# The attended product of the first context attention as seven block products, with two general PSUM banks

## The chip, the cores and the metric

The kernel runs on one core of one Trainium2 chip. The metric is the device time of one execution in microseconds (us); lower is better. Five engines work side by side, each through its own instruction queue in program order: TensorE (PE; its weight loads are listed apart as PEld), VectorE (DVE), ScalarE (ACT), GpSimd (POOL) and SyncE (SP), which here only issues transfers. They synchronise by semaphores alone.

## What is computed

Two transformer layers over a state x of 8 batches x 128 tokens x 512. Each has an attention over a context (8 x 2048 x 512), a self attention and a feed-forward part. The change is in the first layer's context attention. Per batch and per head (8 heads, query and key width 64, value width 128):

```python
k = jnp.einsum('bkt,hta->bhka', key_tokens, key_down)
q = jnp.einsum('bqt,hta->bhqa', query_tokens, query_down) + query_down_bias[None]
logits = jnp.einsum('bhka,bhqa->bhkq', k, q)
attn = swishmax(logits, axis=-2)        # x*exp(x-max) / (sum|x*exp(x-max)| + 1)
vs = jnp.einsum('bhkq,bkt->bhqt', attn, key_tokens)
vs = jnp.einsum('bhqc,hct->bhqt', jnp.einsum('bhqt,htc->bhqc', vs, value_down), value_up)
return vs.sum(axis=1)
```

The fifth line, weights (keys x queries) times context tokens (keys x 512), is the attended product. All data is float32.

## The kernel before

`perceiver` runs one function per part of the layers, each a block of its own with one instruction stream per engine. `swishmax_context` is the first. It works in **units**: unit u is batch b = u // 4 and a pair of heads g = u % 4, 32 units in all (NU). Each unit has four **chunks** c of 512 keys, so there are 128 steps n = 4u + c. `pe_step`, `act_step` and `dve_step` write out by hand what each engine does in step n:

- `key` (for the next unit): keys of the pair from the transposed context, 4 matmuls of 512 columns into a general bank, copied out by ACT.
- `score`: 2 matmuls into two score banks of their own, one per head. DVE takes the maximum (`max`), ACT the exponential (`exp`), DVE multiplies by the score (`weigh`), ACT sums the absolute values (`abs`), DVE scales (`scale`).
- `turned` (for the unit before): the weights of each head are transposed, 4 transposes of 128 x 128 into a general bank. Head 0 is copied out by ACT, head 1 by DVE, into `weights_t`, which holds two chunks.
- `attend` (for the chunk of n - LAG, LAG = 5): the attended product of one chunk. For 4 key tiles k and 4 column tiles m a matmul takes the context tile as stationary operand and 256 columns of weights (two heads x 128 queries): 16 matmuls, accumulated over the four chunks in two banks `attended`.
- `values` (after the fourth chunk): ACT and DVE copy one `attended` bank each to `values_t`, after which the next unit's `attend` may start over.
- `inner` (once a unit): 8 matmuls of 128 columns with `value_down`; `output` (once a batch): 8 matmuls of 512 columns with `value_up`, which DVE adds to x. `hidden` and `query` prepare the queries of the next batch.

The order on PE inside a step is score, key, turned (both heads), inner where there is one, attend, and then hidden, query or output where there is one. The four general banks are handed out in turn by `SharedRing`: whoever fills a bank waits until what stood in it four places earlier has been copied out (`evicted(before)`). PSUM has eight banks: four general, two `attended`, two `score`.

In the profile a float32 matmul appears as two MATMUL and two LDWEIGHTS instructions, and a transpose as one of each; so the 16 matmuls of `attend` are x32. Context chunks are loaded by POOL into `context` (one batch, a chunk overwritten as soon as the last unit of the batch before has attended it), transposed context and weights by SP. All of `value_down` and `value_up` lie in SBUF.

After this stage come two self attentions (`token_attention`, called "twin" and "plain"), the experts, the second layer's context attention and the rest. In both self attentions some tiles `ahead` of the second context attention are computed first, from `ahead.stream` and `ahead.w`.

## Time and profile before

| | us |
|---|---|
| median of 3 runs | 4236.43 |
| lowest and highest run | 4236.34, 4237.85 |
| the profiled execution | 4237.23 |
| span of its trace, first to last instruction | 4235.4 |
| of it, first stage (swishmax_context) | 0 to about 1755 |

| engine | busy, us | share |
|---|---|---|
| PE | 4116.7 | 97% |
| PEld | 2772.9 | 65% |
| DVE | 1982.7 | 47% |
| ACT | 1402.7 | 33% |
| POOL | 240.6 | 6% |

A row of the timeline merges equal instructions that follow one another: its start, the time from the first start to the last end, the engine, the line, what is written and read, and their count (x). A PE row runs on for some hundredths to a tenth of a microsecond after the next has begun, because matmuls are pipelined; so the time from one row's start to the next row's start is what a piece of work takes on PE. "idle before" in square brackets is the engine's idle time ahead of a row and what ended it.

### The profile page before, as it was taken

The numbers are of one execution on the slowest core, as the hardware profiler recorded it, in microseconds if no ns is written. First come the engines' busy times: TensorE is split into PE (matmuls) and PEld (weight loads), VectorE is DVE, ScalarE is ACT, GpSimd is POOL, SyncE is SP. The second block draws the span as 40 slices with busy tenths as digits, with TensorE's granted clock in tenths as the row PEclk, the third lists the DMA queues.
The fourth block names the chain that finished last, engine by engine and source line by source line (L and its number), as shares of the span: only waits on it lengthen the run. The fifth ranks groups of instructions, "written<-read, shape, count | busy, mean of one in ns | idle before, by whom it ended". The sixth has DMA issues, their size and how long they took to land. (4 is left out here: it accounts for less than half of the span.)

```text
span 4235.4 us, 62228 instructions
## 1 busy us (share of the span) xinstructions
PE 4116.7 (97%) x25216; PEld 2772.9 (65%) x25216; DVE 1982.7 (47%) x4077; ACT 1402.7 (33%) x3796; POOL 240.6 (6%) x247
## 2 busy tenths in 40 slices
PE   9999999999999999999899999999999999999897
PEld 5767676767777677677466444666666666676675
DVE  4333333333333333245544233666666666656556
ACT  3222222222222222144333100444444444434343
POOL 0000000000000000012210000000000000000122
PEclk9999999999999999999999999999999999999999
DMA  5011111111111111201120500101101101101000
GB/s 180 30 49 32 40 40 40 40 40 40 40 40 40 40 40 40 85 21 41 54 90 22 184 0 25 50 15 53 45 24 53 43 26 53 43 11 43 11 2 21
DMA packets 86435, 189.71 MB, mean 45 GB/s; under 512 B 7696, under 2 KB 17552, under 8 KB 84368
## 3 DMA queue, kind: packets, MB, share of 16 engines
q1 hardware_dynamic: 72976, 137.55, 9.7%
...
q14 instruction: 71, 0.58, 0.0%
...
## 5 line engine op out<-in xcount | busy, mean ns | idle before, releaser
L502 PE MATMUL swishmax_attended<-swishmax_weights_t,swishmax_context 128*128 128x256 f32 x4096 | 905.1, 379 | 0.0
L502 PEld LDWEIGHTS swishmax_attended<-swishmax_weights_t,swishmax_context 128*128 128x128 f32 x4096 | 768.4, 190 | 99.2
L517 PE MATMUL swishmax_bank<-ahead_stream,swishmax_w_key 128*128 128x512 f32 x1024 | 474.9, 607 | 7.4 <-DMA ahead_stream<-in_context_t_dram 7.4
L1427 PE MATMUL context_bank<-ahead_stream,ahead_staged 128*128 128x512 f32 x1024 | 473.0, 605 | 1.3 <-PEq L1000 1.3
L1293 ACT ACTIVATE context_exps<-context_score,context_neg_max 128x512 f32<-128x512 f32 x512 | 344.7, 685 | 379.4 <-DVE context_neg_max L1325 379.4
L383 ACT ACTIVATE swishmax_xes<-swishmax_score,swishmax_neg_max 128x512 f32<-128x512 f32 x256 | 164.5, 687 | 836.4 <-DVE swishmax_neg_max L415 836.4
L517 PEld LDWEIGHTS swishmax_bank<-ahead_stream,swishmax_w_key 128*128 128x128 f32 x1024 | 184.9, 190 | 287.2 <-issue 284.1
L1427 PEld LDWEIGHTS context_bank<-ahead_stream,ahead_staged 128*128 128x128 f32 x1024 | 184.2, 189 | 280.8 <-issue 273.9
L415 DVE TENSOR_REDUCE swishmax_neg_max<-swishmax_score 128x1 f32<-128x512 f32 x256 | 165.0, 686 | 432.2 <-PE swishmax_score L488 432.2
L1325 DVE TENSOR_REDUCE context_neg_max<-context_score 128x1 f32<-128x512 f32 x512 | 317.8, 683 | 104.8 <-PE context_score L1395 104.1
L1442 PEld LDWEIGHTS context_bank<-whole_ident,context_exps 128*128 128x128 f32 x2048 | 229.1, 141 | 119.1 <-issue 69.5
L1442 PE MATMUL context_bank<-whole_ident,context_exps 128*128 128x128 f32 x2048 | 276.2, 277 | 17.7 <-ACT context_weights_t L1311 11.4
L1436 PE MATMUL context_bank<-ahead_w,ahead_stream 128*128 128x128 f32 x2304 | 269.0, 275 | 0.0
L1436 PEld LDWEIGHTS context_bank<-ahead_w,ahead_stream 128*128 128x128 f32 x2304 | 263.3, 192 | 1.9 <-issue 1.9
L1342 DVE TENSOR_SCALAR context_exps<-context_exps,context_scale 128x512 f32<-128x512 f32 x512 | 213.4, 481 | 1.1
L1311 ACT COPY context_weights_t<-context_bank 128x512 f32<-128x512 f32 x308 | 177.6, 588 | 105.8 <-PE context_bank L1442 104.8
L455 DVE COPY swishmax_weights_t<-swishmax_bank 128x512 f32<-128x512 f32 x128 | 88.5, 691 | 226.1 <-PE swishmax_bank L523 226.1
L420 DVE TENSOR_TENSOR swishmax_xes<-swishmax_xes,swishmax_score 128x512 f32<-128x512 f32 x256 | 164.6, 684 | 20.0 <-ACT swishmax_xes L383 20.0
L1363 DVE COPY context_weights_t<-context_bank 128x512 f32<-128x512 f32 x204 | 141.0, 691 | 48.9 <-PE context_bank L1442 34.2
L523 PEld LDWEIGHTS swishmax_bank<-whole_ident,swishmax_xes 128*128 128x128 f32 x1024 | 119.6, 141 | 66.7 <-issue 66.3
L391 ACT ACTIVATE swishmax_unused<-swishmax_xes 128x512 f32<-128x512 f32 x256 | 160.3, 636 | 0.0
L1395 PE MATMUL context_score<-context_keys_t,context_queries_t 32*128 32x512 f32 x1024 | 147.2, 645 | 0.9 <-DVE context_queries_t L1367 0.9
...
## 6 DMA issues: line engine op xcount, KB each, us to landing
ahead_stream<-in_context_t_dram SPq DMA_DIRECT2D x78, 1024.0 KB, 5.5
swishmax_context<-in_context_dram POOLq DMA_DIRECT2D x32, 1024.0 KB, 5.8
ahead_values<-ahead_staged SPq DMA_DIRECT2D x14, 1024.0 KB, 8.4
...
swishmax_up<-in_L_xattn_value_up_dram SPq DMA_DIRECT2D x1, 2048.0 KB, 10.1
```

The costliest lines, as they stand in the source:

```text
L383: nc.scalar.activation(xes[:, n % XES, r, :], score[r][:], ACT.Exp, bias=neg_max[:, e, r, c:c + 1]).then_inc(exped, 1)
L415: nc.vector.tensor_reduce(neg_max[:, e, r, c:c + 1], score[r][:], AX.X, ALU.max, negate=True).then_inc(maxed, 1)
L420: nc.vector.tensor_tensor(xe, xe, score[r][:], ALU.mult).then_inc(weighted, 1)
L502: last = nc.tensor.matmul(attended[m // 2][:, m % 2, :], context[:, c, k, m * P:(m + 1) * P], weights_t[:, n % 2, k].rearrange("p r q -> p ...
L517: last = nc.tensor.matmul(bank_t[:], w_key[:, k, g * P:(g + 1) * P], context_t[:, c, k, :], start=k == 0, stop=k == DC - 1)
L1293: nc.scalar.activation(exps[:, n % EXPS, r, :], score[r][:], ACT.Exp, bias=neg_max[:, u % 2, r, c:c + 1], accum_out=total[:, u % 2, r, c:c ...
L1311: nc.scalar.copy(weights_t[:, n % 2, r], ring.bank(t)[:].rearrange("p (k q) -> p k q", q=P)).then_inc(out_a, 1)
L1325: nc.vector.tensor_reduce(neg_max[:, e, r, c:c + 1], score[r][:], AX.X, ALU.max, negate=True).then_inc(maxed, 1)
L1342: nc.vector.tensor_scalar(exps[:, slot, r, :], exps[:, slot, r, :], scale[:, e, r, c:c + 1], None, ALU.mult).then_inc(scaled, 1)
L1427: last = nc.tensor.matmul(bank_t[:], w["k"][:, k, g * P:(g + 1) * P], context_t[:, c, k, :], start=k == 0, stop=k == DC - 1)
L1436: last = nc.tensor.matmul(bank_t[:, m * P:(m + 1) * P], context_t[:, c, k, m * P:(m + 1) * P], w["v"][:, k, g * P:(g + 1) * P], start=k == ...
L1442: last = nc.tensor.transpose(bank_t[:, k * P:(k + 1) * P], exps[:, n % EXPS, r, k * P:(k + 1) * P], ident[:])
```

## The change

**Seven products.** The weights of a chunk (512 keys x two heads of 128 queries) and the context (512 keys x 512 columns) are each cut into four blocks: key halves, heads, and halves of the columns. The four block outputs (two column halves x two heads) are formed from seven block products instead of eight (the Winograd form of Strassen's scheme). Each product is 2 key tiles x 2 column tiles, a matmul of 128 columns each: 28 matmuls of 128 columns in place of 16 of 256. They accumulate over the four chunks in four `attended` banks, two products to a bank and one in the last.

**Sums of the context** (S1, S2, S4 in a new tile `sides`, S3 in place of one quarter of `context`): four GpSimd instructions of 512 columns per chunk and batch, in `combine_sides`.

**Sums of the weights** (T1 to T4): in the `turned` step of DVE. The transposes are now grouped by head block so that ACT copies B11 and B21 and DVE reads B12 and B22 from its bank: one copy and four sums of 256 columns in place of one copy of 512.

**Sums of the products:** at the end of a unit ACT copies the first bank (products 1 and 2) to `pair`; GpSimd adds its halves (`first_value`), DVE does six sums of 256 columns. `values_t` has one buffer, not two.

**PSUM:** two general banks instead of four, since `attended` takes four. On PE the two `turned` of a step now stand on either side of `key`; on ACT `turned` stands between the two `exp`. `output` is done per unit (2 matmuls) one step after `inner`.

**SBUF:** to make room, `value_down` and `value_up` are loaded per unit in slabs of two heads (two slabs), the key weights lie in `ahead.w` and `ahead.w` itself is loaded near the end of the stage, and `xes` has 5 places, not 6. In both self attentions the weights share one semaphore, so the first query waits for all of them.

The diff, cut to its core:

```diff
+    KEYS, XES = 6, 5
+
+    A11, A12, A22, S1, S2, S3, S4 = range(7)
+    B11, B21, B22, T1, T3, T2, T4 = range(7)
+    PRODUCTS = ((A11, B11), (A12, B21), (S4, B22), (S1, T1), (S3, T3), (S2, T2), (A22, T4))
...
-        w_key = s.sb("w_key", [P, DC, H * A])
+        w_key = ahead.w
...
-        down = s.sb("down", [P, H, DC, C])
-        up = s.sb("up", [P, H, D])
+        down = s.sb("down", [P, 2, HG, DC, C])
+        up = s.sb("up", [P, 2, HG, D])
...
+        sides = s.sb("sides", [P, NCH, 3, 2, D // 2])
...
-        weights_t = s.sb("weights_t", [P, 2, DC, HG, P])
+        weights_t = s.sb("weights_t", [P, 2, 7, 2, P])
...
-        values_t = s.sb("values_t", [P, 2, DC, HG * P])
-        inner_t = s.sb("inner_t", [P, H, P])
+        values_t = s.sb("values_t", [P, DC, HG, P])
+        pair = s.sb("pair", [P, 2, 2, P])
+        partial = s.sb("partial", [P, 3, 2, P])
+        inner_t = s.sb("inner_t", [P, 2, HG, P])
...
-        bank = [s.ps(f"bank{n}", [P, CH]) for n in range(4)]
-        attended = [s.ps(f"attended{n}", [P, 2, HG * P]) for n in range(2)]
+        bank = [s.ps(f"bank{n}", [P, CH]) for n in range(2)]
+        attended = [s.ps(f"attended{n}", [P, 2, 2, P]) for n in range(4)]
...
+        def product(i):
+            return attended[i // 2][:, i % 2]
+
+        def side(which, c, k, m):
+            if which in (S1, S2, S4):
+                return sides[:, c, (S1, S2, S4).index(which), k, m * P:(m + 1) * P]
+            lower, right = which in (A12, A22), which in (A22, S3)
+            return context[:, c, 2 * lower + k, 2 * right * P + m * P:2 * right * P + (m + 1) * P]
...
-            out = [("key", 0, c + 1)] * (u == 0 and c + 1 < NCH) + [("score", u, c)] * (u < NU) + [("key", u + 1, c)] * (u + 1 < NU)
-            out += [("turned", u - 1, c, r) for r in range(HG)] * (1 <= u <= NU)
+            out = [("key", 0, c + 1)] * (u == 0 and c + 1 < NCH) + [("score", u, c)] * (u < NU)
+            out += [("turned", u - 1, c, 0)] * (1 <= u <= NU) + [("key", u + 1, c)] * (u + 1 < NU) + [("turned", u - 1, c, 1)] * (1 <= u <= NU)
             out += [("inner", (n - LAG) // NCH - 1)] * (n - LAG >= NCH and (n - LAG) % NCH == 0)
+            out += [("output", (n - LAG) // NCH - 1)] * (n - LAG >= NCH and (n - LAG) % NCH == 1)
             out += [("attend", (n - LAG) // NCH, (n - LAG) % NCH)] * (0 <= n - LAG < NU * NCH)
-            out += [("hidden", b + 1)] * (g == 2 and c == 1 and b + 1 < B) + [("query", b + 1)] * (g == 2 and c == 2 and b + 1 < B)
-            return out + [("output", b - 1)] * (g == 1 and c == 2 and b >= 1)
+            return out + [("hidden", b + 1)] * (g == 2 and c == 1 and b + 1 < B) + [("query", b + 1)] * (g == 2 and c == 2 and b + 1 < B)
...
-            out += [("exp", u, c, r) for r in range(HG)] * (u < NU) + [("key", u + 1, c)] * (u + 1 < NU)
-            out += [("turned", u - 1, c, 0)] * (1 <= u <= NU)
+            out += [("exp", u, c, 0)] * (u < NU) + [("turned", u - 1, c, 0)] * (1 <= u <= NU)
+            out += [("exp", u, c, 1)] * (u < NU) + [("key", u + 1, c)] * (u + 1 < NU)
...
+                def load_slab(u):
+                    g = u % NG
+                    for r in range(HG):
+                        sp.dma_start(down[:, u % 2, r], a["value_down"][HG * g + r].rearrange("(t p) c -> p t c", p=P)).then_inc(slab_landed[u % 2], 16)
+                    sp.dma_start(up[:, u % 2], a["value_up"][HG * g:HG * g + HG].rearrange("h c d -> c h d")).then_inc(slab_landed[u % 2], 16)
...
+                    if c == NCH - 1:
+                        if u >= 2:
+
+                            sp.wait_ge(full_d, ring.count(("output", u - 2)))
...
+                def combine_sides(b, c):
+                    pool.wait_ge(ctx_landed[c], 16 * (b + 1))
+                    a11, a12, a21 = context[:, c, 0:2, 0:2 * P], context[:, c, 2:4, 0:2 * P], context[:, c, 0:2, 2 * P:]
+                    a22 = context[:, c, 2:4, 2 * P:]
+                    s1, s2, s4 = (sides[:, c, n] for n in range(3))
+                    link(nc.gpsimd.tensor_tensor(s1, a21, a22, ALU.add))
+                    link(nc.gpsimd.tensor_tensor(s2, s1, a11, ALU.subtract))
+                    link(nc.gpsimd.tensor_tensor(s4, a12, s2, ALU.subtract))
+                    nc.gpsimd.tensor_tensor(a21, a11, a21, ALU.subtract).then_inc(sided, 1)
+
+                def first_value(u):
+                    pool.wait_ge(values_out_a, u + 1)
+                    nc.gpsimd.tensor_tensor(values_t[:, 0:2, 0, :], pair[:, 0], pair[:, 1], ALU.add).then_inc(values_out_p, 1)
+
                 for b in range(B):
-                    for c in range(NCH):
-                        if b:
-
-                            pool.wait_ge(attended_chunk, (b * NG - 1) * NCH + c + 1)
-                        else:
-                            pool.wait_ge(ctx_t_landed[NCH - 2], 16)
-                        pool.dma_start(context[:, c], ctx_dram[b * NCH + c].rearrange("(k p) d -> p k d", p=P)).then_inc(ctx_landed[c], 16)
+                    fetch(b, 0)
+                    fetch(b, 1)
+                    combine_sides(b, 0)
+                    fetch(b, 2)
+                    combine_sides(b, 1)
+                    fetch(b, 3)
+                    if b:
+                        first_value(b * NG - 1)
+                    combine_sides(b, 2)
+                    combine_sides(b, 3)
+                    for g in range(NG - 1):
...
-                        nc.scalar.copy(values_t[:, e, 0:2, :], attended[0][:]).then_inc(values_out_a, 1)
+                        nc.scalar.copy(pair[:], attended[0][:]).then_inc(values_out_a, 1)
...
-                        nc.vector.tensor_copy(values_t[:, e, 2:4, :], attended[1][:]).then_inc(values_out_d, 1)
+                        dve.wait_ge(values_out_a, u + 1)
+                        p3, p5, p7, p6, p4 = (product(i) for i in range(2, 7))
+                        u2, u3, u4 = (partial[:, i] for i in range(3))
+                        link(nc.vector.tensor_tensor(u2, pair[:, 0], p6, ALU.add))
+                        nc.vector.tensor_tensor(u3, u2, p7, ALU.add)
+                        link(nc.vector.tensor_tensor(u4, u2, p5, ALU.add))
+                        nc.vector.tensor_tensor(values_t[:, 0:2, 1, :], u4, p3, ALU.add)
+                        nc.vector.tensor_tensor(values_t[:, 2:4, 0, :], u3, p4, ALU.subtract)
+                        nc.vector.tensor_tensor(values_t[:, 2:4, 1, :], u3, p5, ALU.add).then_inc(values_out_d, 1)
...
-                            n, r = u * NCH + t[2], t[3]
-                            last = nc.vector.tensor_copy(weights_t[:, n % 2, :, r, :], ring.bank(t)[:].rearrange("p (k q) -> p k q", q=P))
+                            n = u * NCH + t[2]
+                            w = weights_t[:, n % 2]
+                            b12, b22 = (ring.bank(t)[:, 2 * h * P:2 * (h + 1) * P].rearrange("p (k q) -> p k q", q=P) for h in range(2))
+                            link(nc.vector.tensor_copy(w[:, B22], b22))
+                            dve.wait_ge(out_a, ring.count(("turned", u, t[2], 0)))
+                            nc.vector.tensor_tensor(w[:, T1], b12, w[:, B11], ALU.subtract)
+                            link(nc.vector.tensor_tensor(w[:, T3], w[:, B22], b12, ALU.subtract))
+                            dve.sem_inc(out_d, 1)
+                            link(nc.vector.tensor_tensor(w[:, T2], w[:, B22], w[:, T1], ALU.subtract))
+                            nc.vector.tensor_tensor(w[:, T4], w[:, T2], w[:, B21], ALU.subtract).then_inc(combined, 1)
+                            continue
...
-                        evicted(("turned", u, c, 1))
-                        pe.wait_ge(ctx_landed[c], 16 * (b + 1))
+                        pe.wait_ge(combined, n + 1)
+                        pe.wait_ge(sided, b * NCH + c + 1)
...
-                        for k in range(DC):
-                            for m in range(DC):
-                                last = nc.tensor.matmul(attended[m // 2][:, m % 2, :], context[:, c, k, m * P:(m + 1) * P],
-                                                        weights_t[:, n % 2, k].rearrange("p r q -> p (r q)"),
-                                                        start=c == 0 and k == 0 and m % 2 == 0,
-                                                        stop=c == NCH - 1 and k == DC - 1 and m % 2 == 1)
+                        for i, (left, right) in enumerate(PRODUCTS):
+                            for k in range(2):
+                                for m in range(2):
+                                    last = nc.tensor.matmul(product(i)[:, m, :], side(left, c, k, m), weights_t[:, n % 2, right, k, :],
+                                                            start=c == 0 and k == 0 and m == 0 and i % 2 == 0,
...
-                        pe.wait_ge(values_out_a, u + 1)
+                        pe.wait_ge(values_out_p, u + 1)
...
-                        evicted(("inner", u * NG + NG - 1))
-                        pe.wait_ge(ahead.w_loaded, 32)
-                        for h in range(H):
-                            last = nc.tensor.matmul(bank_t[:], inner_t[:, h, :], up[:, h, :], start=h == 0, stop=h == H - 1)
+                        evicted(("inner", u))
+                        for r in range(HG):
+                            last = nc.tensor.matmul(bank_t[:], inner_t[:, u % 2, r, :], up[:, u % 2, r, :], start=r == 0, stop=r == HG - 1)
...
-                        pe.wait_ge(w_loaded[what[0]], 16)
+                        pe.wait_ge(w_loaded, w_loads)
+                        if twin and what == "query":
```

How the instructions stand, word for word. TensorE, unit 0's `inner` step, the kernel before:

```order
L488 MATMUL swishmax_score<-swishmax_keys_t,swishmax_queries_t 128x512 x2
L517 MATMUL swishmax_bank<-ahead_stream,swishmax_w_key 128x512 x4
L523 MATMUL swishmax_bank<-whole_ident,swishmax_xes 128x128 x8
L530 MATMUL swishmax_bank<-swishmax_values_t,swishmax_down 128x128 x8
L502 MATMUL swishmax_attended<-swishmax_weights_t,swishmax_context 128x256 x16
```

and the same step of the changed kernel (here a matmul and a transpose count once each):

```order
L603 MATMUL swishmax_bank<-whole_ident,swishmax_xes 128x128 x4
L597 MATMUL swishmax_bank<-ahead_stream,ahead_w 128x512 x4
L603 MATMUL swishmax_bank<-whole_ident,swishmax_xes 128x128 x4
L610 MATMUL swishmax_bank<-swishmax_values_t,swishmax_down 128x128 x8
L583 MATMUL swishmax_attended<-swishmax_weights_t,swishmax_context 128x128 x8
L583 MATMUL swishmax_attended<-swishmax_weights_t,swishmax_sides 128x128 x8
L583 MATMUL swishmax_attended<-swishmax_weights_t,swishmax_context 128x128 x4
L583 MATMUL swishmax_attended<-swishmax_weights_t,swishmax_sides 128x128 x4
L583 MATMUL swishmax_attended<-swishmax_weights_t,swishmax_context 128x128 x4
```

Half of the transposes now stand between `key` and `inner`, where all of them stood before, and the 16 matmuls of 256 columns have become 28 of 128.

VectorE from the last `scale` of a unit's fourth attended chunk to the next step, before:

```order
L438 TENSOR_SCALAR swishmax_xes<-swishmax_xes,swishmax_scale 128x512 x2
L442 COPY swishmax_values_t<-swishmax_attended 128x512
L415 TENSOR_REDUCE swishmax_neg_max<-swishmax_score 128x1 x2
L420 TENSOR_TENSOR swishmax_xes<-swishmax_xes,swishmax_score 128x512 x2
L455 COPY swishmax_weights_t<-swishmax_bank 128x4x128
```

and in the changed kernel:

```order
L506 TENSOR_TENSOR swishmax_partial<-swishmax_pair,swishmax_attended 128x256
L507 TENSOR_TENSOR swishmax_partial<-swishmax_partial,swishmax_attended 128x256
L508 TENSOR_TENSOR swishmax_partial<-swishmax_partial,swishmax_attended 128x256
L509 TENSOR_TENSOR swishmax_values_t<-swishmax_partial,swishmax_attended 128x2x128
L510 TENSOR_TENSOR swishmax_values_t<-swishmax_partial,swishmax_attended 128x2x128
L511 TENSOR_TENSOR swishmax_values_t<-swishmax_partial,swishmax_attended 128x2x128
L476 TENSOR_REDUCE swishmax_neg_max<-swishmax_score 128x1 x2
L481 TENSOR_TENSOR swishmax_xes<-swishmax_xes,swishmax_score 128x512 x2
L526 COPY swishmax_weights_t<-swishmax_bank 128x256
L528 TENSOR_TENSOR swishmax_weights_t<-swishmax_bank,swishmax_weights_t 128x256
L529 TENSOR_TENSOR swishmax_weights_t<-swishmax_weights_t,swishmax_bank 128x256
L531 TENSOR_TENSOR swishmax_weights_t<-swishmax_weights_t 128x256
```

One copy between two steps has become six sums ahead of the next step's maxima, and one copy of the turned weights a copy and four sums.

## Rows read from the trace of the kernel before

**Rows 1.** The page: busy time, share and instructions; granted clock in 40 slices.

```profile
PE 4116.7 (97%) x25216; PEld 2772.9 (65%) x25216; DVE 1982.7 (47%) x4077; ACT 1402.7 (33%) x3796; POOL 240.6 (6%) x247
...
PEclk9999999999999999999999999999999999999999
```

**Rows 2.** Windows: from:to length, busy us (x) per engine, clock, DMA share, GB/s.

```profile
60.00:1744.00 1684.00, 1683.75 (x7393) 1193.83 (x7392) 593.69 (x1192) 462.23 (x1047) 20.97 (x28) 1.00 0.12 38
1744.00:4235.40 2491.40, 2381.75 (x17664) 1554.93 (x17664) 1363.22 (x2822) 920.92 (x2708) 216.26 (x211) 0.98 0.13 43
```

**Rows 3.** The page's groups: busy us, mean ns of one, idle before.

```profile
L502 PEld LDWEIGHTS swishmax_attended<-swishmax_weights_t,swishmax_context 128*128 128x128 f32 x4096 | 768.4, 190 | 99.2
```

**Rows 4.** Timeline of PE: start us, us, engine, line, what, count; an inner step.

```profile
697.79 1.13 PE L488 MATMUL swishmax_score<-swishmax_keys_t,swishmax_queries_t 64*128 64x512 f32 x4
698.85 3.70 PE L517 MATMUL swishmax_bank<-ahead_stream,swishmax_w_key 128*128 128x512 f32 x8
...
702.39 1.04 PE L523 MATMUL swishmax_bank<-whole_ident,swishmax_xes 128*128 128x128 f32 x8
703.26 1.95 PE L530 MATMUL swishmax_bank<-swishmax_values_t,swishmax_down 128*128 128x128 f32 x16
705.05 7.07 PE L502 MATMUL swishmax_attended<-swishmax_weights_t,swishmax_context 128*128 128x256 f32 x32
712.05 1.13 PE L488 MATMUL swishmax_score<-swishmax_keys_t,swishmax_queries_t 64*128 64x512 f32 x4
```

**Rows 5.** Timeline of ACT in the same step.

```profile
697.90 0.58 ACT L397 COPY swishmax_values_t<-swishmax_attended 128x512 f32<-128x512 f32 x1 [5.48 <-PE swishmax_attended L502]
699.67 1.29 ACT L383 ACTIVATE swishmax_xes<-swishmax_score,swishmax_neg_max 128x512 f32<-128x512 f32 x2 [1.19 <-DVE swishmax_neg_max L415]
702.59 0.59 ACT L400 COPY swishmax_keys_t<-swishmax_bank 128x512 f32<-128x512 f32 x1 [1.63 <-PE swishmax_bank L517]
703.07 0.59 ACT L404 COPY swishmax_weights_t<-swishmax_bank 128x512 f32<-128x512 f32 x1
```

**Rows 6.** Timeline of DVE, the end of this step and the start of the next.

```profile
705.25 0.43 DVE L458 COPY swishmax_inner_t<-swishmax_bank 128x256 f32<-128x256 f32 x1 [1.09 <-PE swishmax_bank L530]
705.59 0.87 DVE L438 TENSOR_SCALAR swishmax_xes<-swishmax_xes,swishmax_scale 128x512 f32<-128x512 f32 x2
713.21 1.29 DVE L415 TENSOR_REDUCE swishmax_neg_max<-swishmax_score 128x1 f32<-128x512 f32 x2 [6.75 <-PE swishmax_score L488]
714.65 1.28 DVE L420 TENSOR_TENSOR swishmax_xes<-swishmax_xes,swishmax_score 128x512 f32<-128x512 f32 x2 [0.16 <-ACT swishmax_xes L383]
```

**Rows 7.** Timeline of PE: long runs of 128-column matmuls in later stages.

```profile
1789.05 7.38 PE L916 MATMUL twin_bank_a<-twin_hidden_t,ahead_stream 128*128 128x128 f32 x64 [0.83 <-ACT ahead_staged L762]
1796.27 7.31 PE L916 MATMUL twin_bank_d<-twin_hidden_t,twin_wk 128*128 128x128 f32 x64
...
3054.16 3.84 PE L1452 MATMUL context_bank<-context_hidden_t,ahead_staged 128*128 128x128 f32 x32
3057.93 1.14 PE L1395 MATMUL context_score<-context_keys_t,context_queries_t 32*128 32x512 f32 x8
```

**Rows 8.** Groups of POOL, shapes apart: busy us, mean ns | idle before.

```profile
L862 POOL TENSOR_TENSOR plain_hidden<-plain_hidden,plain_offset 128x512 f32<-128x512 f32 x8 | 13.1, 1643 | 0.6
...
L871 POOL TENSOR_TENSOR twin_result<-twin_result,twin_gain 128x512 f32<-128x512 f32 x8 | 10.1, 1265 | 49.2 <-DVE twin_result L145 49.2
```

**Rows 9.** Timeline at the end of the first stage, PE and DVE.

```profile
1744.85 2.02 PE L530 MATMUL swishmax_bank<-swishmax_values_t,swishmax_down 128*128 128x128 f32 x16 [0.99 <-DVE swishmax_values_t L442]
...
1743.90 0.69 DVE L442 COPY swishmax_values_t<-swishmax_attended 128x512 f32<-128x512 f32 x1 [13.12 <-PE swishmax_attended L502]
```

**Rows 10.** The plain self attention: last weight load (issue, landing) and first query.

```profile
2112.53 2.29 SPq L191 DMA_DIRECT2D plain_wo<-in_L_ffn_Wo_dram  x1
...
plain_wo<-in_L_ffn_Wo_dram SPq DMA_DIRECT2D x1, 1024.0 KB, 15.0
...
2136.26 3.81 PE L916 MATMUL plain_bank_a<-plain_hidden_t,plain_wq 128*128 128x128 f32 x32 [0.83 <-ACT ahead_staged L762]
```

84 lines of the change are left out of this document (50 added, 34 removed).

## The prediction

> **What bounds the kernel now.** I read the page first: PE is busy for 97% of the span at full granted clock in practically every slice [rows 1]. Then a table by stage: in the steady part of the first stage, 60 to 1744 us, PE is busy 1683.75 of 1684.00 us, while DVE has 594, ACT 462 and POOL 21 us of work [rows 2]. So there PE waits for nobody, and the stage lasts as long as PE's own instructions follow one another. What PE is spared there is gained whole, and what it must wait for that it need not wait for now is lost whole. Then the timeline of one step, for the price of each piece as the time from its start to the next piece's start [rows 4]: score 1.06 us (697.79 to 698.85), key 3.54 (to 702.39), the eight transposes 0.87 (to 703.26), inner 1.79 (to 705.05), attend 7.00 (to 712.05). Last the same step on ACT and DVE, for where they stand when PE will need them [rows 5, 6].
>
> **The product.** It takes 7.00 us for 32 instructions of 256 columns, 0.219 each [rows 4]. The new one is 28 matmuls, 56 instructions of 128 columns. For that form the nearest rows are: 16 in 1.79 us in inner, 0.112 each [rows 4]; 64 in 7.22 us (1789.05 to 1796.27), 0.1128 each; 32 in 3.77 us (3054.16 to 3057.93), 0.1178 each [rows 7]. The new run is 56 long and unbroken, so the run of 64 is its nearest relative: 56 x 0.1128 = 6.32 us. The saving is 0.68 us a step, times 128 steps = **-87.0 us**; by the other two it would be 0.73 (-93) and 0.40 (-51). An eighth fewer columns would be 0.87 us; the rest is lost because the shorter matmul pays more beside its columns.
>
> **The sums of the weights.** DVE's part of turned grows from one copy of 512 to one copy and four sums of 256 columns. The row for 256 columns is 0.43 us [rows 6], four to five of them with their waits about 2.2 us. The chunk attended in a step is the one turned a step before, so a whole attend, over 6 us, lies between. DVE is idle for 6.75 us at the end of such a step [rows 6]. Cost 0. If that cover were gone, each further microsecond would be one on PE, 128 times.
>
> **Two general banks.** This is where PE starts to wait. With four banks nobody met one that was not yet copied out. With two, inner needs the bank that key filled two places before, and so does output a step later; the transposes and the next key find banks that were copied out long before. From rows: ACT starts the key copy 3.74 us after key starts (698.85 to 702.59) and takes 0.59 [rows 4, 5]; with some 0.06 us to wake PE (estimate from gaps between a copy's end and its follower) the bank is free 4.39 us after key's start. PE arrives after key and half of the transposes, 3.54 + 0.44 = 3.98. It waits 0.41 us, in 32 inner and 32 output steps: 64 x 0.40 = **+25.6 us**. Lower bound 0 (if the wait vanished in the pipeline), upper bound 0.5 each, +32, if PE must also reload a weight that it could not fetch ahead.
>
> **The sums of the products.** After a unit's fourth chunk DVE now has six sums where it had one copy, all ahead of the next step's maxima, and behind the maxima hang exp on ACT, then ACT's turned, exp and key copies. With time 0 at the start of the next score: ACT's copy of the pair runs from 0.11 (697.90 less 697.79) to 0.70 [rows 4, 5]. The first sum starts at 0.73. A dependent 256-column operation follows after about 0.46 us, an independent one after 0.34 (0.43 less the overlap of about 0.09 that the pair of 0.48 us scales in 0.87 us shows [rows 6]), so two dependent and four independent steps give 2.28 us, and the first max starts at 3.01 instead of 1.16 (713.21 less 712.05 [rows 4, 6]). Then exp of head 0 at 3.73, ACT's turned copy 4.33 to 4.92, second exp 4.83 to 5.52, key copy 5.42 to 6.00, PE woken at 6.06. PE wants the bank of the second half of the transposes at 1.06 + 0.44 + 3.54 = 5.04, which is free at 4.98: no wait, by a hair. It wants the key bank for inner at 5.48: it waits 0.58 us and not 0.40. So 32 x 0.18 = **+5.8 us**. The sums themselves (end 3.1) and GpSimd's (one addition of 256 columns, under 1.3 us, since 512 take 1.27 [rows 8]) are due at 5.48 and are hidden.
>
> **Sums of the context.** Four POOL instructions of 512 columns at 1.27 to 1.64 us [rows 8], 5 to 6.6 us a chunk, 32 chunks. They start when a chunk has landed; attend of that chunk of the new batch is four steps, some 50 us, after the buffer came free. Queued behind them on POOL are the next fetch and `first_value`; the fetch of chunk 3 waits for the last attend anyway, and `first_value` stands ahead of the last two chunks' sums. Cost 0; up to +10 us in all if a DVE chain is disturbed at the seven batch ends. Here the 1.64 us row shows one thing: the same POOL addition took 0.38 us longer than its twin of 1.27 in another phase. The Trainium skill (SBUF — State Buffer, Who interferes with whom) says that VectorE and GpSimd share a pair of ports and that one of them blocks wholly while a two-port VectorE instruction runs. Taken at its word a scale of DVE could stand still for one whole POOL instruction; this is 1.3 us against 6.75 idle, so the sum by that rule stays the same, except in the product sums, whose operands come partly from PSUM.
>
> **The rest.** Output is cut into 32 runs of 4 instructions where it had 8 runs of 16: the same columns, and some 0.1 us at 24 more seams, **+2.4**. At the end of the stage PE waits 0.99 us for one DVE copy that starts at 1743.90 [rows 9]; now it waits for the pair copy and the sums, 0.04 + 0.59 + 0.03 + 2.4 + 0.06 = 3.1 us: **+2.2**. The turned split around key keeps the number of seams: 0, at most 0.1 x 128 = 13. The slab loads have two units' time. Weight loads under one semaphore: in the plain phase the last is issued at 2112.53 and lands 15.0 us later, at 2128, and the first query runs at 2136.26 [rows 10]: 8 us of cover by the tiles ahead; cost 0.
>
> **Sum:** -87.0 + 25.6 + 5.8 + 2.4 + 2.2 = **-51 us**. The profiled execution took 4237.2 (span 4235.4), 0.8 over the median; 4237.2 - 51 = 4186.2, and against the median **4185 us**, -1.2%.
>
> **Rivals.**
>
> *A: the two banks cost nothing.* Then only seams remain: -87 + 5 = -82, 4154 us. For it: 0.4 us is a small figure, put together from starts and ends. Against: the key copy cannot start before key has ended, and only 0.44 us of transposes follow.
>
> *B: the product sums hold up the second transposes (slower).* The place is the step after each unit's last attend. The bank that ACT's turned copy frees is due at 5.04 and free at 4.98, so every microsecond by which DVE's chain is longer than reckoned goes to PE, 32 times. If all six sums went at the pace of dependent 512-column ones (0.69 + 0.04), the chain would be 4.4 us instead of 2.28, +2.1 x 32 = +67 us: 4252. It is level when the chain takes 1.6 us more, and slower by over 0.2% from 1.9 us more. For it: several waits stand in the chain, and POOL works beside it. Against: 256 columns took 0.43 us, not 0.69 [rows 6]. A chain 0.5 to 1 us longer gives 4200 to 4217.
>
> *C: the weight loads pace the product.* A weight load record lasts 190 ns [rows 3], and the new product has 56 of them instead of 32, each over a matmul of half the length. If they did not overlap, a product would take 56 x 0.19 = 10.6 us, +3.6 x 128, some 4650 us. The point of no gain is 0.125 us an instruction. The runs of 64 contradict it: same loads, 0.1128 [rows 7]. The Trainium skill (TensorE: Matmul & The Clock Gate, Back-to-back issue gap) says that the spacing of matmuls is set by the weight load as well and that short ones suffer, which speaks against this change; by that rule its time would be this rival's, but the rows above are of this very form.
>
> That the change doesn't do what it says is excluded by the order of the instructions.
>
> **How the numbers follow.** The forecast, with bank waits of 0.2 to 0.6 us, 4168 to 4200: chance 0.62. A, 4150 to 4168: 0.12. The milder B, 4200 to 4228: 0.14. B in full: 0.07, of it 0.03 within 0.2% and 0.04 slower. C: 0.02. The rest 0.03, something in the start of the stage or in GpSimd's sums, on the slower side as often as level. The range leaves out the ends of A, the upper part of mild B, full B and C: **4154 to 4216**. What a measurement of this kernel can tell from no change is about 0.2%, 8.5 us. Faster by more 0.88, within 0.05, slower 0.07.
>
> **What would show it.** From one attend row's start to the next row's start 6.3 us (over 7.0 is C). Idle time of PE ahead of inner and output, ended by ACT's key copy, 0.4 to 0.6 us each, 64 times; none is A. Idle time ahead of the second transposes, ended by ACT's turned copy, is B. The first max after a unit 3.0 us after the score's start. PE's wait ahead of the last inner 3 us. The granted clock stays at 2.4 GHz in the stage; drops after the new waits would make the prediction wrong, and so would a wait ended by POOL.

## The result and the profile after

The changed kernel takes 4212.49 us (median of 5 runs, 4211.15 to 4213.39) against 4236.57 us (5 runs, 4236.34 to 4239.4): ratio 0.9942, 95% interval 0.9931 to 0.9952. It is 24.1 us faster; 51 were forecast, with a range down to 21. The direction came out and the size did not, and the profile says where the other half stayed.

The page of the profile after, its first line and the two groups of the product (answering [rows 1, 3]; the product now reads either context tiles or the sums in `sides`):

```profile
PE 4053.0 (96%) x28288; PEld 2813.3 (67%) x28288; DVE 2247.2 (53%) x4773; ACT 1401.1 (33%) x3796; POOL 427.8 (10%) x407
...
L583 PE MATMUL swishmax_attended<-swishmax_weights_t,swishmax_context 128*128 128x128 f32 x4096 | 522.1, 276 | 0.0
...
L583 PE MATMUL swishmax_attended<-swishmax_weights_t,swishmax_sides 128*128 128x128 f32 x3072 | 385.5, 275 | 0.0
```

PE is busy 64 us less, but the span shrank by only 26 (4235.4 to 4209.3). So PE now waits, in a kernel where it waited almost nowhere. Windows of the first stage show in which stretches (columns as in [rows 2]: from:to, length, busy us of PE, PEld, DVE, ACT and POOL, granted clock, DMA share, GB/s):

```profile
60.00:69.00 9.00, 3.87 (x12) 1.61 (x10) 8.37 (x31) 0.93 (x2) 0.00 (x0) 0.96 0.00 0
69.00:76.00 7.00, 6.71 (x36) 6.71 (x37) 3.89 (x9) 2.53 (x7) 0.00 (x0) 0.57 0.00 1
...
82.00:1681.00 1599.00, 1575.99 (x10137) 1191.84 (x10136) 834.08 (x1825) 453.41 (x1032) 186.56 (x170) 1.00 0.19 61
1681.00:1690.00 9.00, 6.57 (x45) 6.36 (x44) 5.41 (x14) 1.07 (x2) 0.73 (x1) 0.81 0.00 0
...
1717.00:1740.00 23.00, 17.26 (x46) 9.11 (x44) 11.88 (x43) 1.13 (x3) 0.72 (x1) 0.70 0.20 74
```

The long middle has 23 us of idle PE, spread over 1599. The first row has 5 us in 9, and the clock of the next one, 0.57, says that PE spent most of it at the lower level (1.2 of 2.4 GHz). The end of the stage repeats this twice. To turn windows into a balance I took the starts of `score` on PE, one a step, and cut both stages at the same steps (the 9th and the 121st score; the first matmul of the next stage as the end). The last column is what the prediction's own terms give for each stretch.

| stretch | before, us | after, us | difference | due by the forecast |
|---|---|---|---|---|
| start to 9th score | 91.1 | 102.4 | +11.3 | -2.0 |
| 9th to 121st score | 1523.1 | 1479.0 | -44.0 | -46.7 |
| 121st score to end of stage | 141.6 | 149.3 | +7.7 | -2.4 |
| all later stages | 2479.7 | 2478.6 | -1.0 | 0 |
| sum | 4235.4 | 4209.3 | -26.1 | -51.1 |

Due are 3, 112 and 13 `attend` of -0.68 us, and the bank waits, seams and the end's wait where they fall. The steady part is right within 3 us. Two short stretches, together 6% of the kernel, ate 23 us.

**The steady step.** Timeline of PE (start, us, engine, line, what, count, [idle before <- releaser]); first a plain step, then the piece of an inner step around its wait, answering [rows 4]:

```profile
724.69 1.13 PE L568 MATMUL swishmax_score<-swishmax_keys_t,swishmax_queries_t 64*128 64x512 f32 x4
725.75 0.66 PE L603 MATMUL swishmax_bank<-whole_ident,swishmax_xes 128*128 128x128 f32 x4
726.24 3.60 PE L597 MATMUL swishmax_bank<-ahead_stream,ahead_w 128*128 128x512 f32 x8
729.67 0.60 PE L603 MATMUL swishmax_bank<-whole_ident,swishmax_xes 128*128 128x128 f32 x4
730.11 1.95 PE L583 MATMUL swishmax_attended<-swishmax_weights_t,swishmax_context 128*128 128x128 f32 x16
...
736.46 1.13 PE L568 MATMUL swishmax_score<-swishmax_keys_t,swishmax_queries_t 64*128 64x512 f32 x4
...
753.22 0.64 PE L603 MATMUL swishmax_bank<-whole_ident,swishmax_xes 128*128 128x128 f32 x4
754.27 2.05 PE L610 MATMUL swishmax_bank<-swishmax_values_t,swishmax_down 128*128 128x128 f32 x16 [0.41 <-ACT swishmax_keys_t L461]
756.16 1.95 PE L583 MATMUL swishmax_attended<-swishmax_weights_t,swishmax_context 128*128 128x128 f32 x16
```

From score to score it is 11.77 us where it was 12.47 (14.26 less the 1.79 of inner [rows 4]), so a plain step gains 0.70; `attend` takes 6.35 (730.11 to 736.46), forecast 6.32. An inner step takes 14.27 where it took 14.26: it gains 0.70 and loses 0.71 beyond its 1.79, ahead of line 610. An output step takes 13.99: 2.22 over a plain step, where its share of the matmuls is 1.72 (a quarter of the 6.87 that an output took in the kernel before), so it loses 0.50.

**Who waits for whom.** PE's waits after, 57 to 1735 us (engine, buffer and line that wait <- what they wait for: us in all, times, longest):

```profile
PE swishmax_bank L610 <- ACT swishmax_keys_t L461: 11.8, 29, 0.4
PE swishmax_bank L627 <- ACT swishmax_keys_t L461: 6.9, 29, 0.2
PE swishmax_bank L610 <- DVE swishmax_values_t L511: 5.7, 2, 3.3
PE swishmax_bank L603 <- ACT swishmax_weights_t L465: 5.6, 2, 5.4
PE swishmax_bank L610 <- ACT swishmax_weights_t L465: 2.8, 1, 2.8
PE swishmax_bank L603 <- DVE swishmax_xes L499: 2.1, 2, 1.8
```

The first two rows are the waits that the prediction named: ACT's key copy, 29 times each instead of 32. The rest are few and long, and they belong to the two short stretches.

**The start.** PE after, the sixth step, and below it what DVE and ACT did meanwhile:

```profile
59.81 0.63 PE L603 MATMUL swishmax_bank<-whole_ident,swishmax_xes 128*128 128x128 f32 x4 [1.76 <-DVE swishmax_xes L499]
60.27 3.60 PE L597 MATMUL swishmax_bank<-ahead_stream,ahead_w 128*128 128x512 f32 x8
69.29 1.12 PE L603 MATMUL swishmax_bank<-whole_ident,swishmax_xes 128*128 128x128 f32 x4 [5.42 <-ACT swishmax_weights_t L465]
70.20 3.62 PE L583 MATMUL swishmax_attended<-swishmax_weights_t,swishmax_context 128*128 128x128 f32 x16
73.61 2.62 PE L583 MATMUL swishmax_attended<-swishmax_weights_t,swishmax_sides 128*128 128x128 f32 x16
...
59.97 4.25 DVE L158 BATCH_NORM_STATS2 swishmax_x_stats<-whole_x 128x6 f32<-128x512 f32 x7
...
67.35 1.29 DVE L476 TENSOR_REDUCE swishmax_neg_max<-swishmax_score 128x1 f32<-128x512 f32 x2
...
68.08 0.69 ACT L441 ACTIVATE swishmax_xes<-swishmax_score,swishmax_neg_max 128x512 f32<-128x512 f32 x1 [9.67 <-DVE swishmax_neg_max L476]
68.66 0.58 ACT L465 COPY swishmax_weights_t<-swishmax_bank 128x512 f32<-128x512 f32 x1
```

Read it from below: PE's second transposes (69.29) want the bank that ACT empties at 68.66; ACT does that after exp of head 0 (68.08), which needs DVE's maximum (67.35), and ahead of that DVE computes the normalization statistics of batches 1 to 7 in one piece, 59.97 to 67.35. PE stands still for 5.42 us, and then runs 16 instructions in 3.41 us (70.20 to 73.61) and the next 16 in 2.46, where 1.79 is the pace at full clock. The step takes 21.92 us where it took 12.97; the one before it 8.63 where it took 6.19, since transposes now stand ahead of key and wait for a scale.

**The end.** PE after, the waits of the last two units (the middle ones left out), answering [rows 9]:

```profile
1646.52 2.05 PE L610 MATMUL swishmax_bank<-swishmax_values_t,swishmax_down 128*128 128x128 f32 x16 [2.82 <-ACT swishmax_weights_t L465]
...
1685.43 3.14 PE L610 MATMUL swishmax_bank<-swishmax_values_t,swishmax_down 128*128 128x128 f32 x16 [2.44 <-DVE swishmax_values_t L511]
...
1721.36 3.75 PE L610 MATMUL swishmax_bank<-swishmax_values_t,swishmax_down 128*128 128x128 f32 x16 [3.31 <-DVE swishmax_values_t L511]
1725.72 3.75 PE L627 MATMUL swishmax_bank<-swishmax_up,swishmax_inner_t 128*128 128x512 f32 x4 [0.61 <-DVE swishmax_inner_t L535]
```

In the last unit there is no key for a next one, and after it no score. So the 3.5 us of key that had covered the chain pair copy, sums, maxima, exp, turned copy are gone, while the chain is as long as before. The last wait of 3.31 us was forecast as 3.1; that the next 20 instructions would run at half clock, twice 3.75 us for what takes 1.95 and 1.9, was not.

### The profile page after: what moved, and what is told of

The parts are those of the page before. It is cut to its first block and busy times, and to the rows that moved or that the text cites. A ratio compares the mean times of both kernels' runs of the same rounds, so it can differ in the third digit from the quotient of the medians.

```text
span 4209.3 us, 69698 instructions
## 1 busy us (share of the span) xinstructions
PE 4053.0 (96%) x28288; PEld 2813.3 (67%) x28288; DVE 2247.2 (53%) x4773; ACT 1401.1 (33%) x3796; POOL 427.8 (10%) x407
## 5 line engine op out<-in xcount | busy, mean ns | idle before, releaser
L583 PE MATMUL swishmax_attended<-swishmax_weights_t,swishmax_context 128*128 128x128 f32 x4096 | 522.1, 276 | 0.0
L583 PEld LDWEIGHTS swishmax_attended<-swishmax_weights_t,swishmax_context 128*128 128x128 f32 x4096 | 492.7, 193 | 14.8 <-issue 14.8
L597 PE MATMUL swishmax_bank<-ahead_stream,ahead_w 128*128 128x512 f32 x1024 | 463.8, 596 | 7.6 <-DMA ahead_stream<-in_context_t_dram 7.6
L441 ACT ACTIVATE swishmax_xes<-swishmax_score,swishmax_neg_max 128x512 f32<-128x512 f32 x256 | 177.3, 694 | 843.2 <-DVE swishmax_neg_max L476 843.2
L583 PE MATMUL swishmax_attended<-swishmax_weights_t,swishmax_sides 128*128 128x128 f32 x3072 | 385.5, 275 | 0.0
L583 PEld LDWEIGHTS swishmax_attended<-swishmax_weights_t,swishmax_sides 128*128 128x128 f32 x3072 | 364.4, 192 | 0.0
L597 PEld LDWEIGHTS swishmax_bank<-ahead_stream,ahead_w 128*128 128x128 f32 x1024 | 185.8, 191 | 196.8 <-issue 194.6
L481 DVE TENSOR_TENSOR swishmax_xes<-swishmax_xes,swishmax_score 128x512 f32<-128x512 f32 x256 | 175.6, 687 | 66.8 <-ACT swishmax_xes L441 66.8
L603 PE MATMUL swishmax_bank<-whole_ident,swishmax_xes 128*128 128x128 f32 x1024 | 161.0, 281 | 10.8 <-ACT swishmax_weights_t L465 5.6
## 6 DMA issues: line engine op xcount, KB each, us to landing
whole_x<-in_x_dram SPq DMA_DIRECT2D x8, 256.0 KB, 10.9
```

Of the source, the lines that this page charges most:

```text
L441: nc.scalar.activation(xes[:, n % XES, r, :], score[r][:], ACT.Exp, bias=neg_max[:, e, r, c:c + 1]).then_inc(exped, 1)
L481: nc.vector.tensor_tensor(xe, xe, score[r][:], ALU.mult).then_inc(weighted, 1)
L583: last = nc.tensor.matmul(product(i)[:, m, :], side(left, c, k, m), weights_t[:, n % 2, right, k, :], start=c == 0 and k == 0 and m == 0 a ...
L597: last = nc.tensor.matmul(bank_t[:], w_key[:, k, g * P:(g + 1) * P], context_t[:, c, k, :], start=k == 0, stop=k == DC - 1)
L603: last = nc.tensor.transpose(bank_t[:, k * P:(k + 1) * P], xes[:, n % XES, r, k * P:(k + 1) * P], ident[:])
```

## The experiments

Two theories stood at the start. **Cover**: the loss is PE waiting for chains on DVE and ACT at the two ends, since with two banks transposes, inner and output meet a bank still in use; moving work on DVE or PE gives it back. **Contention**: GpSimd's sums, or the product itself, cost something in every step. All runs share the runs of the kernel before made in the same batch (medians 4236.7 to 4238.2).

**Statistics out of the way.** DVE gathers the statistics of batches 1 to 7 a step after the first `attend`, finishes them one step later, and the normalizations follow them.

```diff
-            out += [("stats", 1)] * (n == NCH) + [("norm", b + 1)] * (g == 1 and c == 2 and b + 1 < B)
+            out += [("gather", 1)] * (n == NCH + 2) + [("finish", 1)] * (n == NCH + 3) + [("norm", b + 1)] * (g == 2 and c == 0 and b + 1 < B)
```

> The changed kernel, but the row statistics of batches 1 to 7 on DVE (7.4 us in one piece, between steps 4 and 5) are cut in two and put behind steps 6 and 7; norm of batch 1 follows two steps later. Theory start-and-end (the 128-step middle went as forecast, the missing 27 us stand at the start and the end of the stage): PE's wait of 5.4 us ahead of the second transposes at 69.3 us and the half-clock stretch behind it go, 8 to 10 us less than 4212.5, so about 4203. Rival spread (GpSimd and DVE contention or seams in every step): 4212, no change.

4204.57 us (4202.6 to 4206.21), ratio 0.9924 (0.9908 to 0.9941), 7.9 faster than the change. PE in the step of the long wait:

```profile
61.11 3.60 PE L602 MATMUL swishmax_bank<-ahead_stream,ahead_w 128*128 128x512 f32 x8
64.55 0.60 PE L608 MATMUL swishmax_bank<-whole_ident,swishmax_xes 128*128 128x128 f32 x4
64.99 1.95 PE L588 MATMUL swishmax_attended<-swishmax_weights_t,swishmax_context 128*128 128x128 f32 x16
```

The second transposes follow key at once, the product's first 16 instructions take 1.95 instead of 3.62, and the step takes 13.57 instead of 21.92. The mechanism is shown. The total needs more care: the 9th score comes 7.5 us earlier, which is 8.35 from this step and 1.6 from a first score that happens to start earlier, less 2.45 in the step before it (11.08 instead of 8.63; the run without GpSimd's sums, below, shows where part of that comes from). The moved normalization makes seven steps 0.46 longer (15.17 instead of 14.71), and the stage ends only 2.9 earlier. Of the 8.5 between the two spans the other 5.6 lie in later stages whose instructions are the same; the section on the hardware comes back to them.

**Inner and output behind attend.** On PE they follow `attend` in their step, on DVE their copies follow the scales.

```diff
-            out += [("inner", (n - LAG) // NCH - 1)] * (n - LAG >= NCH and (n - LAG) % NCH == 0)
-            out += [("output", (n - LAG) // NCH - 1)] * (n - LAG >= NCH and (n - LAG) % NCH == 1)
             out += [("attend", (n - LAG) // NCH, (n - LAG) % NCH)] * (0 <= n - LAG < NU * NCH)
+            out += [("inner", (n - LAG) // NCH - 1)] * (n - LAG >= NCH and (n - LAG) % NCH == 0)
+            out += [("output", (n - LAG) // NCH - 1)] * (n - LAG >= NCH and (n - LAG) % NCH == 1)
```

> The changed kernel, but inner and output stand behind attend on PE (and behind scale on DVE), so that the key bank has long been copied out when they want it. Bank-wait theory: an inner step loses 0.7 us and an output step 0.48 us beyond their matmuls, 31 times each, 36 us in all, plus 2.8 + 0.95 + some of 2.4 us near the end of the stage; these go: 4170 to 4176. Rival: the wait only moves, to the next step's key or transposes, which then find the bank of inner or output not yet copied out: 4205 to 4215.

4172.74 us (4171.59 to 4174.61), ratio 0.9848 (0.9832 to 0.9864), 39.8 faster than the change. PE's waits, 82 to 1640 us, are all that is left there:

```profile
PE swishmax_attended L583 <- DVE swishmax_values_t L511: 1.1, 1, 1.1
PE swishmax_bank L603 <- DVE swishmax_xes L499: 0.4, 1, 0.4
PE swishmax_bank L603 <- ACT swishmax_weights_t L465: 0.2, 1, 0.2
```

An inner step now takes 13.60 and an output step 13.49; 32 times the 0.67 and the 0.50 saved is 37. In the last unit the steps take 11.47 and 10.05 instead of 13.21 and 11.26. So the bank waits are the whole loss of the steady part, and 6.3 us of product in front of inner are enough to hide ACT's key copy and DVE's chain both.

**Both.** The two edits together.

> Both edits, statistics moved and inner and output behind attend. If both theories hold and the parts are independent: the sum of their gains, 4160 to 4168, 1.7% under the kernel before. Rival: as the better of the two alone.

4162.68 us (4160.21 to 4169.94), ratio 0.983 (0.9813 to 0.9846). The sum of the two single gains, 47.7, gives 4164.8: they add. This version beats both kernels; the next ones only polish it.

**A short chain.** Three of the six sums of products on DVE are left out.

```diff
-                        link(nc.vector.tensor_tensor(u2, pair[:, 0], p6, ALU.add))
-                        nc.vector.tensor_tensor(u3, u2, p7, ALU.add)
-                        link(nc.vector.tensor_tensor(u4, u2, p5, ALU.add))
-                        nc.vector.tensor_tensor(values_t[:, 0:2, 1, :], u4, p3, ALU.add)
-                        nc.vector.tensor_tensor(values_t[:, 2:4, 0, :], u3, p4, ALU.subtract)
-                        nc.vector.tensor_tensor(values_t[:, 2:4, 1, :], u3, p5, ALU.add).then_inc(values_out_d, 1)
+                        nc.vector.tensor_tensor(values_t[:, 0:2, 1, :], pair[:, 0], p3, ALU.add)
+                        nc.vector.tensor_tensor(values_t[:, 2:4, 0, :], pair[:, 0], p4, ALU.subtract)
+                        nc.vector.tensor_tensor(values_t[:, 2:4, 1, :], pair[:, 0], p5, ALU.add).then_inc(values_out_d, 1)
```

> The changed kernel with three of the six DVE sums of the products left out (u2, u3, u4; the three that write the values stay, so part of the computation is missing). The chain ahead of the next maxima is 1.3 us shorter. Forecast's term: PE's wait ahead of inner falls from 0.41 to 0.24 us, 31 times, 5 us, and 1.3 us at each of the waits near the end: about 4204. Rival that the sums cost nothing because inner waits for the key copy anyway: 4210 to 4212. Rival that the chain is the main loss: under 4195.

4202.57 us (4199.89 to 4203.75), ratio 0.9919 (0.9902 to 0.9936). An inner step takes 14.06 instead of 14.27, and the first step of the last unit without key 11.96 instead of 13.21. With the sums shorter the inner step gives back 0.21 us, the 0.18 that the prediction had charged for them; its other 0.5 stays, and is the bank's. Where key is missing PE gets back 1.25 us, about the length of three sums: the waits of 2.82, 2.44 and 3.31 us at the end become 1.57, 1.19 and 2.06. The stretch from the 121st score to the end of the stage takes 141.8 us instead of 149.3. Of these 7.5 us the waits are 3.75; nearly all of the rest is that the clock stays up behind them, and that much happens without the shorter chain too, in the run without GpSimd's sums below.

**Before with two banks.** The kernel before, with two general banks and the order of the change on PE and ACT, the product as it was.

```diff
-        bank = [s.ps(f"bank{n}", [P, CH]) for n in range(4)]
+        bank = [s.ps(f"bank{n}", [P, CH]) for n in range(2)]
...
-            out += [("turned", u - 1, c, r) for r in range(HG)] * (1 <= u <= NU)
+            out += [("turned", u - 1, c, 0)] * (1 <= u <= NU) + [("key", u + 1, c)] * (u + 1 < NU) + [("turned", u - 1, c, 1)] * (1 <= u <= NU)
```

> The kernel before, with two general banks instead of four and the changed kernel's order on PE and ACT (transposes on both sides of key, turned between the exps); the product stays as it was, inner ahead of attend, output behind it once a batch. Theory start-and-end: 32 inner waits of 0.4 to 0.7 us (13 to 22 us) and 8 to 14 us at the start and end of the stage behind DVE's statistics and ACT's copies: 4260 to 4270. Rival, that the start and end losses come from the longer sums and not from the banks: 4250 to 4255.

4255.96 us (4250.54 to 4257.19) against 4236.7, ratio 1.0044 (1.0027 to 1.006). The long wait at the start is there, to the hundredth, without any product of seven:

```profile
67.20 1.12 PE L523 MATMUL swishmax_bank<-whole_ident,swishmax_xes 128*128 128x128 f32 x4 [5.42 <-ACT swishmax_weights_t L404]
68.11 9.05 PE L502 MATMUL swishmax_attended<-swishmax_weights_t,swishmax_context 128*128 128x256 f32 x32
```

The product behind it takes 9 us instead of 7.00, and the 9th score comes at 102.0 instead of 91.1. So 10.9 of the 13.3 us that the start lost against the forecast come from the banks and their order alone. An inner step takes 14.72 instead of 14.26, +0.46; over a plain step of the same kernel (12.43) and its 1.79 it is 0.50, for the bank alone, forecast 0.40. The end is another matter: from the 121st score to the end of the stage this kernel takes 143.3 us, only 1.7 over the kernel before, where the change takes 7.7 more. The total lies between the two expectations, nearer the rival's, and each was half right: the start is the banks', and the end needs the longer sums too.

**Before with 128 columns.** The kernel before, each matmul of the product split in two, so 64 instructions of 128 columns instead of 32 of 256.

```diff
-                                last = nc.tensor.matmul(attended[m // 2][:, m % 2, :], context[:, c, k, m * P:(m + 1) * P],
-                                                        weights_t[:, n % 2, k].rearrange("p r q -> p (r q)"),
...
+                                for r in range(HG):
+                                    last = nc.tensor.matmul(attended[m // 2][:, m % 2, r * P:(r + 1) * P], context[:, c, k, m * P:(m + 1) * P],
+                                                            weights_t[:, n % 2, k, r, :],
...
```

> The kernel before, each attend matmul of 256 columns cut in two of 128: 32 matmuls, 64 instructions, nothing else. Pace of the forecast, 0.111 to 0.113 us an instruction: attend 7.15 to 7.2 us in place of 7.0, 4255 to 4263. Rival that a long run of short matmuls is paced by weight loads (0.118 and more): over 4300.

4267.6 us (4264.53 to 4271.41) against 4236.7, ratio 1.0073 (1.0056 to 1.009), above what was expected. One product:

```profile
702.81 7.31 PE L503 MATMUL swishmax_attended<-swishmax_weights_t,swishmax_context 128*128 128x128 f32 x64
710.05 1.13 PE L488 MATMUL swishmax_score<-swishmax_keys_t,swishmax_queries_t 64*128 64x512 f32 x4
```

64 instructions in 7.24 us are 0.1131 each; 7.24 less 7.00, 128 times, is 30.7, all of the 30.9 measured. An eighth of 7.24 is 0.905, and 7.24 less 0.905 is 6.34, the `attend` of the change. This splits the product's -0.66 cleanly: +0.24 for the shorter form, -0.90 for the eighth product.

**Without GpSimd's sums.** They run for batch 0 only.

```diff
+                    if b:
+                        pool.sem_inc(sided, 1)
+                        return
                     s1, s2, s4 = (sides[:, c, n] for n in range(3))
```

> The changed kernel with GpSimd's sums of the context left out for batches 1 to 7 (those batches use the sums of batch 0; part of the computation is missing). Forecast: they are hidden and disturb nobody: 4212, within 2 us. Rival contention (DVE and GpSimd share ports at each batch end): 4 to 10 us less.

4212.07 us (4209.94 to 4213.31), ratio 0.9943 (0.9927 to 0.996); the change has 4212.49. Some 144 us of GpSimd work are gone and no step of batches 1 to 7 is shorter. So contention costs PE nothing there. But it exists, on DVE. The change at the first batch end, DVE, then one of GpSimd's four additions beside it, and last the DVE row of the same sum without GpSimd's:

```profile
282.65 1.38 DVE L532 TENSOR_TENSOR swishmax_weights_t<-swishmax_weights_t 128x256 f32<-128x256 f32 x1
284.28 2.56 DVE L499 TENSOR_SCALAR swishmax_xes<-swishmax_xes,swishmax_scale 128x512 f32<-128x512 f32 x2
...
282.41 1.33 POOL L409 TENSOR_TENSOR swishmax_sides<-swishmax_sides,swishmax_context 128x512 f32<-128x512 f32 x1
...
283.21 0.42 DVE L535 TENSOR_TENSOR swishmax_weights_t<-swishmax_weights_t 128x256 f32<-128x256 f32 x1
```

At each of the seven batch ends two sums of the weights take 1.2 to 1.5 and 1.4 us (the last time 0.7 and 1.4) instead of 0.42, and two scales 2.56 instead of 0.87, 2.9 to 3.7 us in all; the sums that read PSUM keep their 0.42. DVE is idle for 2.19 us behind it where it was idle for 5.92, and so PE sees nothing of it.

At the start it does. There batch 0's sums, which this run keeps, meet the chain of small DVE operations that the first transposes wait for: the sum into `total` takes 0.61 us in the change and 1.25 here, and the second operation after it 0.17 and 1.11, where the kernel before takes 0.17 for each; they end when the GpSimd addition beside them ends. PE's wait ahead of these transposes is 2.63 us in the kernel before with two banks, which has no such sums, 3.07 in the change, 3.84 with the statistics moved and 4.65 here, and the step takes 11.64 here instead of 8.63. No run of the changed kernel leaves out the sums of batch 0, so their direct price in the change, 0.44 us, is only read from these waits.

The stretches say what the median hides. From the 9th to the 121st score both kernels take 1479.0 us. But the stage ends in 145.7 us here and in 149.3 in the change, with the same instructions and the same waits of 2.82, 2.4, 3.31 and 0.61 us: behind the last two, inner and output take 2.02 and 1.95 us here and 3.75 and 3.75 in the change. The later stages then take 3.1 us more here (2481.7 for 2478.6). So whether the clock falls behind the last waits is not decided by these waits.

**The normalization back.** Both edits, and the normalization moved only in batch 0, where it has to follow the statistics.

```diff
-[("norm", b + 1)] * (g == 2 and c == 0 and b + 1 < B)
+[("norm", b + 1)] * (g == (1 if b else 2) and c == (2 if b else 0) and b + 1 < B)
```

> The kernel with both edits (statistics moved, inner and output behind attend), but norm back in its old step for all batches except batch 1, for which the statistics are too late there. With both edits the inner step that also has hidden takes 14.49 us where it took 14.03 with norm in its old step. If this is norm's 0.54 us ahead of the sums of the products, six steps get 0.46 us shorter: 2.8 us less than 4162.7, about 4160. If it is the split statistics or something of the step itself: no change.

4161.8 us (4161.27 to 4164.58), ratio 0.9824 (0.981 to 0.9837). Six steps take 14.03 instead of 14.49, 2.8 us; 0.9 of it is seen in the median, within the spread of the other's runs.

**A fill for the clock.** The same, and 28 transposes whose result nobody reads, while PE waits for the last sums.

```diff
                     elif what == "inner":
+                        if u == NU - 1:
+                            for k in range(28):
+                                nc.tensor.transpose(score[0][:, 0:P], ident[:], ident[:])
                         pe.wait_ge(values_out_p, u + 1)
```

> The same kernel, and on PE 28 transposes of the identity into a score bank that nobody reads any more, between the last attend and the last inner, where PE waits 3.3 us for the sums of the products; they take 28 x 0.109 = 3.05 us and write nothing that is used. Clock theory: it is this idle time that brings TensorE to 1.2 GHz behind it, where the last inner and output and the start of the next stage run at half speed; with the wait filled the clock stays at 2.4 GHz there and 4 to 6 us go, about 4155. Rival, that the clock falls anyway because of the pauses of 0.6, 1.2 and 0.8 us at the change of stage: within 1 us of the kernel without them.

4160.35 us (4159.47 to 4161.23), ratio 0.9819 (0.9805 to 0.9832), the fastest of all. The same place without the fill, timeline of PE and a window:

```profile
1677.67 3.75 PE L615 MATMUL swishmax_bank<-swishmax_values_t,swishmax_down 128*128 128x128 f32 x16 [3.31 <-DVE swishmax_values_t L511]
1682.03 3.75 PE L632 MATMUL swishmax_bank<-swishmax_up,swishmax_inner_t 128*128 128x512 f32 x4 [0.61 <-DVE swishmax_inner_t L540]
```

```profile
1673.00:1690.00 17.00, 11.88 (x37) 7.33 (x36) 6.42 (x14) 0.59 (x1) 0.73 (x1) 0.61 0.11 29
```

And with it:

```profile
1673.52 3.22 PE L612 MATMUL swishmax_score<-whole_ident 128*128 128x128 f32 x28
1676.83 2.02 PE L618 MATMUL swishmax_bank<-swishmax_values_t,swishmax_down 128*128 128x128 f32 x16
1679.46 1.96 PE L635 MATMUL swishmax_bank<-swishmax_up,swishmax_inner_t 128*128 128x512 f32 x4 [0.61 <-DVE swishmax_inner_t L540]
```

```profile
1674.00:1690.00 16.00, 13.82 (x62) 8.00 (x59) 10.44 (x34) 0.30 (x1) 0.73 (x1) 1.00 0.19 56
1690.00:1700.00 10.00, 7.88 (x15) 3.44 (x16) 2.02 (x10) 1.75 (x4) 0.00 (x0) 0.83 0.97 389
```

The fill fills the wait exactly and the clock stays at 2.4 GHz in this profile: 2.02 and 1.96 instead of 3.75 twice, and from the last run of the product to the first matmul of the next stage 10.00 us instead of 13.67. But of these 3.7 only 1.5 arrive in the median. In the next stage PE waits 2.39 us at 1692, and the clock falls there instead (0.83 in the last row). The second piece of that stage starts 9.5 us after the first with the fill, without it, in the change and in the kernel before: it waits for ACT. Without the fill the first piece runs at half clock, 8.71 us, and the wait is 0.80; with it the first piece takes 7.11 and the wait is 2.39, and from there to the next transposes it is 22.40 us instead of 20.70. So the half clock in the first piece had cost nothing, and its absence makes a longer wait with a drop behind it. The drop was put off, not removed. That the fill is what keeps the clock up is not shown: without GpSimd's sums and without any fill the same two rows are 2.02 and 1.95, behind the same wait of 3.31, and there too the next stage has a wait of 2.41. The median, 1.5 us lower, is all that speaks for the fill. The expectation counted the start of the next stage among what would be gained and had no place for that.

## Why the prediction was wrong in size

**Right.** The bound: PE without waits, so that what it is spared is gained. The product's price, 6.32 forecast and 6.27 to 6.35 measured, from the run of 64 in another stage [rows 7]. The chain of the sums: first max 3.01 us after the score forecast, 3.04 measured (748.23 to 751.27). The sums of the weights and GpSimd's at nothing, from batch 1 on: a scale of DVE does stand still for a GpSimd addition, as the prediction had allowed for, and so do sums of the weights, which it had not; 2.19 us of DVE's idle time are left over it. The bank waits: each step that was named lost what was charged within 0.13 us (inner 0.71 for 0.58; output 0.50 for 0.50, of it 0.10 for a seam). Together -44.0 in the middle for -46.7 due. As a rate, -0.393 a step, or -50.3 over 128 steps: the forecast's sum would be right for a stage that is all middle.

**The step that failed first** is the sentence in *Two general banks*: "the transposes and the next key find banks that were copied out long before". It was worked out in one steady step and applied to all. With two banks the second transposes need the bank of the first, which ACT empties behind exp, so behind DVE's maxima. In the steady step this chain ends 1.9 us before PE comes back from key (ACT's copy ends at 739.51, the transposes start at 741.45). At the start DVE has a single piece of 7.4 us ahead of the maxima. Before it stood on DVE too, and cost nothing, since four banks let PE go on. The price is 13.3 us against what was due: 8.35 in the step that the moved statistics take from 21.92 to 13.57, 2.4 in the step before it, 1.3 more in the same step, where the transposes now stand ahead of key and wait 1.76 us for a scale, and 1.3 in the first score. That last part is chance: its start differs by as much between kernels with the same work ahead of it (22.66, and 21.05 with the statistics moved). The kernel before with two banks shows 10.9. Rival B named exactly this chain, "the second transposes wait for ACT's turned copy", but looked for it behind the product sums, 32 times, and not behind the one long piece of DVE's work. The start was mentioned only as part of a rest of 0.03.

**The second** is the term *end of the stage*, +2.2. It priced the last wait (3.1, measured 3.31) and nothing else. It was 10.1 more: 2.5 and 0.7 where inner and output meet no key in the last unit, 1.9 at the inner after it, and some 5 for the half clock behind the waits of 2.4 and 3.3 us. The cover was key; the prediction should have asked in which steps it is missing. The banks alone are not enough for this loss (1.7 us in the kernel before with two banks); with three sums fewer each of the three longest waits is 1.25 shorter. So what the term had at nothing is the chain of the sums in the other steps where nothing covers it. The 5 us of half clock are partly chance: the kernel without GpSimd's sums has the same waits and loses 3.5 less. The prediction had said that drops of the clock after the new waits would make it wrong, and gave them no price.

**The rivals.** A falls: all 58 waits are there. C falls: 0.1131 an instruction (by its own terms, +3.6 x 128 on 4236, it would have been some 4700, not 4650). The milder B gave 4200 to 4228, and the time is there, but by another mechanism: the chain is 3.04 and not 3.5 to 4 long. A time inside a rival's range doesn't confirm the rival.
